# Fetching the context's rounded halves in the second cross attention, stored by the first

## Chip, cores and metric

The kernel runs on one core of a Trainium2 chip. The metric is the time of one execution on the device, in microseconds.

## What is computed

Six layers in a row work on `x` of shape (8, 64, 256), in float32. Two of them are cross attentions over the same context `ctx_1024` of shape (8, 1024, 256): the first layer, with a mask and a squared-relu norm, and the fourth, with a softmax. Cut to what matters:

```python
def _L0_xattn_ref(iQ, iK, mask, Wq, Wkv, Wo, nbias):          # H = 16, ADIM = 16
    rq = (iQ @ Wq.T).reshape(b, q, H, ADIM)
    kv = (iK @ Wkv.T).reshape(b, s, 2, H, ADIM)
    scores = einsum('bqhd,bshd->bhqs', rq, kv[:, :, 0]) / sqrt(ADIM)   # masked
    ...                                                        # relu, square, norm, values, Wo
def _L1_xattn_ref(query, key, value, w_q, w_k, w_v, w_o):     # 16 heads of 64
    scores = einsum('bhqd,bhkd->bhqk', query @ w_q, key @ w_k) * 64 ** -0.5
    attn = softmax(scores)
    return einsum('bhqk,bhkd->bhqd', attn, value @ w_v) ... @ w_o
x = x + _L0_xattn_ref(_layernorm(x), ctx_1024, mask, ...)
x = x + _L0_attn_ref(...);  x = x + _L0_ffn_ref(...)
x = x + _L1_xattn_ref(_layernorm(x), ctx_1024, ctx_1024, ...)
x = x + _L1_attn_ref(...);  x = x + _L1_ffn_ref(...)
```

## The kernel before

Each layer is a function with one block; inside it each engine has its own hand-written list of work, and semaphores tie the lists together. Products that need float32 precision from the faster float32r matmul are made of three matmuls (`product3`, L185): an operand is split into a rounded half `hi` (a cast, on ScalarE) and the remainder `lo` (raw minus `hi`, on VectorE or GpSimd), and hi x hi, hi x lo and lo x hi are added up.

The first cross attention is `xattn0` (L197). It goes batch by batch over the eight batches. SyncE loads the transposed context `ctxT` in two chunks of 128 features x 1024 positions (`load_chunk`, L261, 512 KB each) into one raw tile, once the halves of the batch before have been taken from it (L283, L284). ScalarE casts a chunk into `ctx_hi[b % 2]` (`split`, L320 to L324), VectorE subtracts into `ctx_lo[b % 2]` (`remainder`, L429 to L432), and TensorE makes keys and values from the halves (`piece`, L507) between the scores and outputs of the batch at work. The halves are two batches deep.

The second is `xattn1` (L1537). The key weights are absorbed into the queries, so the scores are queries against the transposed context itself, called the features, `cT[b % 2]` as `hi` and `lo`; the tiles of even batches are named e_cT, those of odd batches f_cT. The outputs are taken against the untransposed context, called the keys, `cN`. A batch has four groups g of two pairs of heads; G = 4 b + g counts groups, n counts pairs.

- SyncE (L1682 to L1732): per group `put` of two pairs (their probabilities, transposed in blocks by VectorE, go to a table `f_turned_rows` in device memory, 512 KB each, L1693), then `fetch` of the two (four transfers of 128 KB each bring them back into `pT_lo`, L1706). A fetch waits until its put has landed. Behind the fetches of group 2 the keys of the next batch are loaded (`load_keys`, L1573, 1 MB), behind those of group 3 the features of the batch after the next (`load_features`, L1569, 1 MB, into the raw tile `rawT`), for which SyncE first waits that the raw tile has been read (L1726, L1727). All of it is one queue.
- ScalarE: exponentials of the scores (L1600), the cast of fetched probabilities (`high`, L1785), and the casts of keys (L1776) and, in group 2, of features (L1769).
- GpSimd: the remainders of keys (L1749) and of features (`pool_features`, L1595).
- VectorE, for a group: `low` of the pairs fetched two groups ago (L1898), two maxima (L1605), and for each of two pairs the division and the block transpose (L1893).
- TensorE, for group G: scores of two pairs (24 matmuls of 512 columns, from `pe_scores`, L1615), then the outputs of group G - 2 (96 matmuls of 256 columns, `outputs`, L1983), which need the two `low` results. All are instructions of L189.

## Time and profile before

| | us |
|---|---|
| median of 3 runs | 962.04 |
| lowest, highest run | 959.30, 963.83 |
| the profiled execution | 959.08 |
| its span, first to last instruction | 957.4 |
| TensorE busy (matmuls) | 912.9 |
| VectorE busy | 632.9 |
| ScalarE busy | 500.1 |
| GpSimd busy | 196.7 |
| first cross attention, about | 0 to 192 |
| second cross attention, about | 377 to 815 |

The profile is one execution, so everything in it is read against 959.08 us and not against the median. Busy time of TensorE counts overlapping matmuls once. Transfers are not instructions of an engine: SyncE's rows show when a transfer is issued, and its landing is seen in what waits for it.

### The profile page before, as it was taken

Reading aid. Unit: us, or ns where it says so; the run is one execution under the profiler, and the core shown is the slowest. Engines: PE = TensorE matmul, PEld = TensorE weight load, DVE = VectorE, ACT = ScalarE, POOL = GpSimd, SP = SyncE. Lnnn points to the kernel's source line nnn. Section 1 sums busy time; section 2 is a strip of 40 time slices with the busy share of each in tenths; the row PEclk is TensorE's granted clock in tenths of the full one; section 3 lists DMA queues with packets and bytes.
Section 4 is the critical chain, followed back from the end, with each engine's and each line's share of the span. In section 5 each row is a group of like instructions: output and inputs, shape, how many; then the busy total and the mean of one; then the engine's idle time right before and its main releaser. Section 6 shows DMA issues by size and latency. Waiting matters only on the chain. (4 is left out here: it accounts for less than half of the span.)

```text
span 957.4 us, 20196 instructions
## 1 busy us (share of the span) xinstructions
PE 912.9 (95%) x8260; PEld 748.3 (78%) x8260; DVE 632.9 (66%) x866; ACT 500.1 (52%) x721; POOL 196.7 (21%) x190
## 2 busy tenths in 40 slices
PE   9999999888989999979999999999999999998996
PEld 7888888755679998558999999999989976567554
DVE  5667776768733335589897979898989843286221
ACT  5777777543456664655555564646454531312331
POOL 2000000020214441422131231404050211321101
PEclk9999999999979999999999999999999999997998
DMA  5211110020212222538887888787969870999993
GB/s 162 81 59 50 49 50 5 3 67 4 66 46 88 88 88 69 151 108 216 264 204 241 214 250 226 235 232 223 251 210 251 220 211 23 286 321 243 339 339 117
DMA packets 103848, 151.92 MB, mean 159 GB/s; under 512 B 11009, under 2 KB 84434, under 8 KB 103762
## 3 DMA queue, kind: packets, MB, share of 16 engines
q1 hardware_dynamic: 102930, 148.35, 53.5%
q0 software_dynamic: 832, 2.36, 0.8%
q8 instruction: 62, 1.02, 0.4%
q14 instruction: 24, 0.20, 0.1%
HBM read 114.50 MB, written 36.18 MB: 157 GB/s over the span
## 5 line engine op out<-in xcount | busy, mean ns | idle before, releaser
L189 PE MATMUL ps<-f_pT_lo,f_cN_hi 128*128 128x256 f32 x512 | 146.9, 287 | 0.0
L189 PE MATMUL ps<-f_pT_hi,f_cN_hi 128*128 128x256 f32 x512 | 145.2, 284 | 0.7 <-DVE f_pT_lo L1898 0.7
L189 PE MATMUL ps<-f_pT_hi,f_cN_lo 128*128 128x256 f32 x512 | 145.2, 284 | 0.0
L448 DVE SCALAR_TENSOR_TENSOR a_u<-ps,a_floor,a_cap 128x1024 f32<-128x1024 f32 x64 | 79.2, 1279 | 47.3 <-PE ps L543 46.9
L1749 POOL TENSOR_TENSOR f_cN_lo<-e_raw,f_cN_hi 128x512 fp32r<-128x512 f32 x32 | 48.4, 1541 | 260.7 <-ACT f_cN_hi L1776 260.7
L189 PEld LDWEIGHTS ps<-f_pT_hi,f_cN_hi 128*128 128x128 f32 x512 | 96.2, 188 | 4.0 <-DVE f_pT_lo L1898 2.2
L189 PEld LDWEIGHTS ps<-f_pT_hi,f_cN_lo 128*128 128x128 f32 x512 | 97.9, 191 | 0.0
L189 PEld LDWEIGHTS ps<-f_pT_lo,f_cN_hi 128*128 128x128 f32 x512 | 96.2, 188 | 1.0
L359 ACT ACTIVATE a_pr<-a_u,a_nb 128x1024 f32<-128x1024 f32 x64 | 73.8, 1153 | 42.7 <-DVE a_u L448 41.5
L1898 DVE TENSOR_TENSOR f_pT_lo<-f_pT_lo,f_pT_hi 128x1024 fp32r<-128x1024 f32 x64 | 81.1, 1290 | 20.0 <-ACT f_pT_hi L1785 19.9
L1785 ACT CAST f_pT_hi<-f_pT_lo 128x1024 fp32r<-128x1024 f32 x64 | 66.9, 1049 | 50.5 <-DMA f_pT_lo<-f_turned_rows 50.4
L1605 DVE TENSOR_REDUCE e_negmax<-ps 128x1 f32<-128x1024 f32 x64 | 76.6, 1217 | 17.4 <-PE ps L189 17.2
L1600 ACT ACTIVATE xn<-ps,e_negmax 128x1024 f32<-128x1024 f32 x32 | 35.7, 1116 | 95.6 <-DVE e_negmax L1605 95.6
L189 PE MATMUL ps<-e_cT_hi,e_qb_hi 128*128 128x512 f32 (+1 forms) x160 | 60.7, 379 | 4.7 <-ACT xn L1600 3.1
L189 PE MATMUL ps<-e_cT_hi,e_qb_lo 128*128 128x512 f32 (+1 forms) x160 | 59.7, 373 | 0.0
L189 PE MATMUL ps<-e_cT_lo,e_qb_hi 128*128 128x512 f32 (+1 forms) x160 | 59.4, 372 | 0.0
L1044 POOL TENSOR_TENSOR d_w_lo<-d_w,d_w_hi 128x512 fp32r<-128x512 f32 x32 | 41.3, 1289 | 78.0 <-ACT d_w_hi L1071 78.0
L189 PE MATMUL ps<-f_cT_hi,e_qb_lo 128*128 128x512 f32 x128 | 50.4, 394 | 0.0
L189 PE MATMUL ps<-f_cT_lo,e_qb_hi 128*128 128x512 f32 x128 | 50.2, 392 | 0.0
L189 PE MATMUL ps<-f_cT_hi,e_qb_hi 128*128 128x512 f32 x128 | 49.7, 388 | 0.0
L1110 DVE TENSOR_TENSOR d_h_lo<-d_h,d_h_hi 128x512 fp32r<-128x512 f32 x32 | 23.9, 746 | 36.8 <-ACT d_h_hi L1091 36.8
L1600 ACT ACTIVATE xnT<-ps,e_negmax 128x1024 f32<-128x1024 f32 x32 | 35.7, 1117 | 17.4 <-DVE e_negmax L1605 17.4
(414 smaller groups left out, 2193.0 us busy)
## 6 DMA issues: line engine op xcount, KB each, us to landing
f_turned_rows<-f_turned SPq DMA_DIRECT2D x64, 512.0 KB, 4.7
f_pT_lo<-f_turned_rows SPq DMA_DIRECT2D x256, 128.0 KB, 3.3
k_w<-in_L_ffn_W SPq DMA_DIRECT2D x30, 1024.0 KB, 14.6
a_ctxT<-in_ctxT SPq DMA_DIRECT2D x16, 512.0 KB, 4.8
d_w<-in_L_ffn_w SPq DMA_DIRECT2D x32, 256.0 KB, 2.7
e_raw<-in_ctxT SPq DMA_DIRECT2D x8, 1024.0 KB, 7.1
e_raw<-in_ctx SPq DMA_DIRECT2D x32, 256.0 KB, 5.9
k_b<-in_L_ffn_b SPq DMA_DIRECT2D x14, 256.0 KB, 11.8
```

Source lines behind the costliest of these rows:

```text
L189: last = nc.tensor.matmul(out, a[i], b[j], start=start and n == 0, stop=stop and n == 2, skip_group_check=skip)
L359: A.activation(pr[:, n % NP, :], u[:, n % NU, :], ACT.Square, bias=nb[:], scale=HD ** -0.5).then_inc(p_ready, 1)
L448: V.scalar_tensor_tensor(u[:, n % NU, :].rearrange("p (r w) -> p r w", r=RT), core.psum[:, 0:2048].rearrange("p (r w) -> p r w", r=RT)[:, ...
L1044: self.c.nc.gpsimd.tensor_tensor(lo[:], raw[:], hi[:].bitcast(F32), ALU.subtract).then_inc(self.lo[i], 1)
L1110: V.tensor_tensor(self.hp[1][:, f % self.RG, :], self.h[:, f % self.RH, :], self.hp[0][:, f % self.RG, :].bitcast(F32), ALU.subtract).then ...
L1600: nc.scalar.activation(pr[p % NPR], core.ps[p % 2][:], ACT.Exp, bias=negmax[:, p:p + 1], accum_out=total[:, p:p + 1]).then_inc(exp_ready, 1)
L1605: nc.vector.tensor_reduce(negmax[:, p:p + 1], core.ps[p % 2][:], AX, ALU.max, negate=True).then_inc(max_ready, 1)
L1749: nc.gpsimd.tensor_tensor(cN[1][:, ks, cols], raw[:, ks, cols], cN[0][:, ks, cols].bitcast(F32), ALU.subtract).then_inc(n_lo, 1)
L1785: nc.scalar.copy(moved(pT_hi, n), moved(pT_lo, n).bitcast(F32)).then_inc(hi_ready, 1)
L1898: nc.vector.tensor_tensor(moved(pT_lo, n), moved(pT_lo, n).bitcast(F32), moved(pT_hi, n).bitcast(F32), ALU.subtract).then_inc(lo_dve, 1)
```

## The change

`xattn0` gets a table in device memory, `halves_d`, of 2 halves x 8 batches x 2 chunks x 128 x 1024 floats (16.8 MB). Behind every chunk load SyncE stores the `hi` and the `lo` of the same chunk of the batch before (`keep`), two transfers of 512 KB; those of the last batch follow at the end, and SyncE waits for all of them. Before the halves' tiles are written again, ScalarE and VectorE wait for the stores of two batches before.

`xattn1` no longer loads raw features. `load_features` fetches the two halves from the table, two transfers of 1 MB, straight into `cT[b % 2]`. The casts and subtractions of features are gone, with their semaphores; TensorE waits for the landing itself. SyncE's waits on them are gone too; ahead of the load in group 3 it waits until all scores of the current batch are made, since the halves' tile is overwritten.

```diff
@@ -194,7 +194,7 @@
 
 
 
-def xattn0(core, x_d, ctxT_d, maskT_d, wqT_d, wkvT_d, woT_d, nbias_d):
+def xattn0(core, x_d, ctxT_d, maskT_d, wqT_d, wkvT_d, woT_d, nbias_d, halves_d):
     nc = core.nc
     H, HD = 16, 16
     HC = P // HD
@@ -246,6 +246,7 @@
         num_ready, den_psum, wo_in = sem("num_ready"), sem("den_psum"), sem("wo_in")
         v_ones, wo_zero, ident_ready = sem("v_ones"), sem("wo_zero"), sem("ident_ready")
         o_ready, y_psum, x_out = sem("o_ready"), sem("y_psum"), sem("x_out")
+        kept = [sem(f"kept{i}") for i in range(2)]
         split_count = lambda b, c: 2 * DC + DC * (b - 1) + c + 1
         norm = Norm(core, "a")
         ident, x = core.ident, core.x
@@ -262,6 +263,10 @@
 
             def load_mask(b):
                 sp.dma_start(mask_u8[:], maskT_d[b, :, :].rearrange("p (k t) -> p k t", t=T)).then_inc(mask_in, 16)
+
+            def keep(b, c):
+                sp.dma_start(halves_d[0, b, c, :, :], ctx_hi[b % 2][:, c, :].bitcast(F32)).then_inc(kept[b % 2], 16)
+                sp.dma_start(halves_d[1, b, c, :, :], ctx_lo[b % 2][:, c, :].bitcast(F32)).then_inc(kept[b % 2], 16)
 
             w_d = wkvT_d.rearrange("(c p) o -> p c o", p=P)
             sp.dma_start(wkv[:, :, 0:D], w_d[:, :, 0:D]).then_inc(wk_in, 16)
@@ -283,8 +288,15 @@
                     sp.wait_ge(hi_ready, 2 * DC if b == 1 else split_count(b - 1, c))
                     sp.wait_ge(lo_ready, 2 * DC if b == 1 else split_count(b - 1, c))
                     load_chunk(b, c)
+                    keep(b - 1, c)
                 sp.wait_ge(mask_read, b)
                 load_mask(b)
+            for c in range(DC):
+                sp.wait_ge(hi_ready, split_count(B - 1, c))
+                sp.wait_ge(lo_ready, split_count(B - 1, c))
+                keep(B - 1, c)
+            for i in range(2):
+                sp.wait_ge(kept[i], 32 * DC * (B // 2))
 
         @block.gpsimd
         def _(pool):
@@ -321,6 +333,7 @@
                 act.wait_ge(ctx_in[c], 16 * b + 16)
                 if b >= 2:
                     act.wait_ge(kv_psum, PIECES * (b - 1))
+                    act.wait_ge(kept[b % 2], 32 * DC * (b // 2))
                 A.copy(ctx_hi[b % 2][:, c, :], ctxT[:, c, :]).then_inc(hi_ready, 1)
 
             def queries(b):
@@ -428,6 +441,8 @@
 
             def remainder(b, c):
                 dve.wait_ge(hi_ready, split_count(b, c))
+                if b >= 2:
+                    dve.wait_ge(kept[b % 2], 32 * DC * (b // 2))
                 V.tensor_tensor(ctx_lo[b % 2][:, c, :], ctxT[:, c, :], ctx_hi[b % 2][:, c, :].bitcast(F32),
                                 ALU.subtract).then_inc(lo_ready, 1)
 
@@ -1534,7 +1549,7 @@
 
 
 
-def xattn1(core, a, finished, early):
+def xattn1(core, a, finished, early, halves_d):
 
 
     nc = core.nc
@@ -1551,7 +1566,7 @@
         rawT = both[:, 0:DC * S].rearrange("p (c s) -> p c s", s=S)
         raw = both[:, DC * S:DC * S + KT * D].rearrange("p (k d) -> p k d", d=D)
         cT = [[core.sb("e_cT0_" + n, [P, DC, S], F32R, ctx) for n in ("hi", "lo")]]
-        t_in, n_in, t_hi, t_lo = core.sem("e_t_in"), core.sem("e_n_in"), core.sem("e_t_hi"), core.sem("e_t_lo")
+        t_in, n_in = [core.sem(f"e_t{i}_in") for i in range(2)], core.sem("e_n_in")
         NPR = 2
         HALF = HP // 2
         QD = 32
@@ -1566,7 +1581,9 @@
         norm = Norm(core, "e")
 
         def load_features(sp, b):
-            sp.dma_start(rawT[:], a["ctxT"][b, :, :].rearrange("(c p) k -> p c k", p=P)).then_inc(t_in, 16)
+            for i in range(2):
+                sp.dma_start(cT[b % 2][i][:].bitcast(F32), halves_d[i, b, :, :, :].rearrange("c p k -> p c k")
+                             ).then_inc(t_in[b % 2], 16)
 
         def load_keys(sp, b):
             for j in range(4):
@@ -1586,14 +1603,6 @@
             dve.wait_ge(qb_hi, 2 * b + half + 3)
             nc.vector.tensor_tensor(qb[1][:, :, cols], queries_of(b, half), qb[0][:, :, cols].bitcast(F32),
                                     ALU.subtract).then_inc(qb_lo, 1)
-
-        def pool_features(pool, b):
-            hi, lo = cT[b % 2]
-            for i in range(4):
-                c, cols = i // 2, slice(S // 2 * (i % 2), S // 2 * (i % 2 + 1))
-                pool.wait_ge(t_hi, 2 * b + c + 1)
-                nc.gpsimd.tensor_tensor(lo[:, c, cols], rawT[:, c, cols], hi[:, c, cols].bitcast(F32),
-                                        ALU.subtract).then_inc(t_lo, 1)
 
         def act_exponentials(act, b, p):
             act.wait_ge(max_ready, HP * b + p + 1)
@@ -1614,7 +1623,7 @@
 
         def pe_scores(pe, b, p):
             if p == 0:
-                pe.wait_ge(t_lo, 4 * b + 4)
+                pe.wait_ge(t_in[b % 2], 32 * (b // 2) + 32)
             if b == 0 and p % 2 == 0:
                 pe.wait_ge(qb_lo, p // 2 + 1)
             if b >= 1 and p % HALF == 0:
@@ -1707,7 +1716,6 @@
                                      rows[n % SLOTS, :, S // 4 * j:S // 4 * (j + 1)].rearrange("(i k) w -> k i w", k=QD)
                                      ).then_inc(pT_in[n % 2], 16)
 
-                sp.wait_ge(t_lo, 4)
                 load_features(sp, 1)
                 for b, g in groups:
                     G = NG * b + g
@@ -1723,9 +1731,8 @@
                         else:
                             sp.dma_start(wo, a["L1_xattn_w_o"].rearrange("(h p) o -> p h o", p=P)).then_inc(wo_in, 16)
                     if g == 3 and b + 1 < B:
-                        sp.wait_ge(t_hi, 2 * b + 4)
-                        sp.wait_ge(t_lo, 4 * b + 8)
                         if b + 2 < B:
+                            sp.wait_ge(s_psum, HP * (b + 1))
                             load_features(sp, b + 2)
                         else:
                             sp.dma_start(wv, a["L1_xattn_w_v"].rearrange("(c p) o -> p c o", p=P)).then_inc(v_in, 16)
@@ -1739,7 +1746,6 @@
                     ps = slice(2 * i, 2 * i + 2)
                     nc.gpsimd.tensor_tensor(wk2[1][:, ps, :], wk[:, ps, :], wk2[0][:, ps, :].bitcast(F32),
                                             ALU.subtract).then_inc(wk_lo, 1)
-                pool_features(pool, 0)
                 early.gpsimd()
 
                 def keys(b, c):
@@ -1755,19 +1761,11 @@
                     if b >= 1:
                         keys(b, 0)
                         keys(b, 1)
-                    if b + 1 < B:
-                        pool_features(pool, b + 1)
                 pool.wait_ge(wo_hi, 1)
                 nc.gpsimd.tensor_tensor(wo2[1], wo, wo2[0].bitcast(F32), ALU.subtract).then_inc(wo_lo, 1)
 
             @block.scalar
             def _(act):
-                def features(b, c):
-                    act.wait_ge(t_in, 16 * b + 16)
-                    if b >= 2:
-                        act.wait_ge(s_psum, HP * (b - 1))
-                    nc.scalar.copy(cT[b % 2][0][:, c, :], rawT[:, c, :]).then_inc(t_hi, 1)
-
                 def keys(b, c):
                     act.wait_ge(n_in, 64 * b + 64)
                     if b >= 1:
@@ -1828,10 +1826,8 @@
                 weights(3)
                 evict(0)
                 query(3)
-                features(0, 0)
                 evict(1)
                 query(4)
-                features(0, 1)
                 evict(2)
                 first_queries(0)
                 query(5)
@@ -1857,9 +1853,6 @@
                     if g == 2:
                         if b >= 1:
                             keys(b, 1)
-                        if b + 1 < B:
-                            features(b + 1, 0)
-                            features(b + 1, 1)
                     if g == 3 and b + 1 < B:
                         queries(b + 1, 0)
                     if g == 0:
@@ -2873,13 +2866,14 @@
 def program(nc, a, out):
     with ExitStack() as ctx:
         core = Core(nc, ctx)
+        halves = nc.dram_tensor("ctx_halves", (2, B, DC, P, S), F32).ap()
         xattn0(core, a["x"], a["ctxT"], a["maskT"], a["L0_xattn_Wq"], a["L0_xattn_Wkv"], a["L0_xattn_Wo"],
-               a["L0_xattn_nbias"])
+               a["L0_xattn_nbias"], halves)
         memory0(core, a)
         ffn0(core, a)
         finished = core.retire_sems()
         early = Ahead(core, "k", a["L1_ffn_W1"])
-        xattn1(core, a, finished, early)
+        xattn1(core, a, finished, early, halves)
         kept = (early.w1_in, early.zeroed, early.zero_out)
         finished = [s for s in core.retire_sems() if s not in kept]
         attn1_ffn1(core, a, out, early, finished)
```

## Rows read from the trace of the kernel before

**Rows 1.** Stretches: bounds; length, PE, PEld, DVE, ACT, POOL busy; clock, DMA share, GB/s.

```profile
100.00:140.00 40.00, 39.71 (x840) 34.29 (x829) 31.94 (x30) 30.13 (x40) 0.00 (x0) 1.00 0.18 59
...
382.00:386.00 4.00, 4.00 (x10) 1.81 (x11) 0.69 (x1) 2.81 (x5) 0.28 (x1) 1.00 1.06 391
...
427.20:430.60 3.40, 3.40 (x10) 2.66 (x9) 3.15 (x5) 2.98 (x5) 0.00 (x0) 0.51 0.44 141
...
451.65:723.77 272.12, 271.82 (x1730) 247.43 (x1729) 236.06 (x251) 150.65 (x204) 71.86 (x48) 1.00 0.83 232
...
555.00:560.00 5.00, 5.00 (x27) 4.25 (x26) 3.75 (x4) 2.66 (x4) 0.00 (x0) 1.00 1.00 338
```

**Rows 2.** Odd batches' feature tiles by instruction: duration ns min/median/max, first and last start.

```profile
L1595 POOL TENSOR_TENSOR f_cT_lo<-e_raw,f_cT_hi x16: 1282/1521/2257, 431.1 to 714.3; 128x512 fp32r<-128x512 f32 x16
L1769 ACT CAST f_cT_hi<-e_raw x8: 1042/1044/1051, 430.0 to 706.7; 128x1024 fp32r<-128x1024 f32 x8
```

**Rows 3.** `low` by duration; and TensorE's waits: us in total, times, longest.

```profile
L1898 DVE TENSOR_TENSOR f_pT_lo<-f_pT_lo,f_pT_hi x64: 1181/1215/2309, 431.0 to 781.7; 128x1024 fp32r<-128x1024 f32 x64
...
PE ps L189 <- ACT xn L1600: 3.1, 1, 3.1
...
PE ps L189 <- DVE f_pT_lo L1898: 0.7, 2, 0.4
```

**Rows 4.** Batch 1's chunks in the first attention: issue, landing of L261, casts.

```profile
9.41 0.82 SPq L261 DMA_DIRECT2D a_ctxT<-in_ctxT  x2
...
DMA to landing us min/median/max: 4.4/4.7/6.1
...
18.09 2.00 ACT L324 CAST a_ctx_hi<-a_ctxT 128x1024 fp32r<-128x1024 f32 x2
```

**Rows 5.** One batch change: landing of all puts (L1693), SyncE's issues, ScalarE's cast.

```profile
DMA to landing us min/median/max: 2.6/4.7/8.5
...
551.83 0.40 SPq L1569 DMA_DIRECT2D e_raw<-in_ctxT  x1
552.45 2.51 SPq L1693 DMA_DIRECT2D f_turned_rows<-f_turned  x2
560.32 3.94 SPq L1706 DMA_DIRECT2D f_pT_lo<-f_turned_rows  x8
...
564.88 1.05 ACT L1785 CAST f_pT_hi<-f_pT_lo 128x1024 fp32r<-128x1024 f32 x1 [3.02 <-DMA f_pT_lo<-f_turned_rows]
```

**Rows 6.** VectorE's second `low` of group 0, six batches: start, duration.

```profile
476.14 1.48 DVE L1898 TENSOR_TENSOR f_pT_lo<-f_pT_lo,f_pT_hi 128x1024 fp32r<-128x1024 f32 x1 [0.76 <-ACT f_pT_hi L1785]
...
523.39 1.69 DVE L1898 TENSOR_TENSOR f_pT_lo<-f_pT_lo,f_pT_hi 128x1024 fp32r<-128x1024 f32 x1 [1.79 <-ACT f_pT_hi L1785]
...
568.25 1.23 DVE L1898 TENSOR_TENSOR f_pT_lo<-f_pT_lo,f_pT_hi 128x1024 fp32r<-128x1024 f32 x1 [1.07 <-ACT f_pT_hi L1785]
...
612.06 1.46 DVE L1898 TENSOR_TENSOR f_pT_lo<-f_pT_lo,f_pT_hi 128x1024 fp32r<-128x1024 f32 x1 [0.79 <-ACT f_pT_hi L1785]
...
657.82 2.23 DVE L1898 TENSOR_TENSOR f_pT_lo<-f_pT_lo,f_pT_hi 128x1024 fp32r<-128x1024 f32 x1 [1.27 <-ACT f_pT_hi L1785]
...
704.43 1.56 DVE L1898 TENSOR_TENSOR f_pT_lo<-f_pT_lo,f_pT_hi 128x1024 fp32r<-128x1024 f32 x1 [0.68 <-ACT f_pT_hi L1785]
```

**Rows 7.** TensorE's first output matmul of the same groups: start, duration.

```profile
479.78 0.28 PE L189 MATMUL ps<-f_pT_hi,f_cN_hi 128*128 128x256 f32 x1
...
525.13 0.39 PE L189 MATMUL ps<-f_pT_hi,f_cN_hi 128*128 128x256 f32 x1
...
570.44 0.28 PE L189 MATMUL ps<-f_pT_hi,f_cN_hi 128*128 128x256 f32 x1
...
615.65 0.28 PE L189 MATMUL ps<-f_pT_hi,f_cN_hi 128*128 128x256 f32 x1
...
660.89 0.28 PE L189 MATMUL ps<-f_pT_hi,f_cN_hi 128*128 128x256 f32 x1
...
706.11 0.33 PE L189 MATMUL ps<-f_pT_hi,f_cN_hi 128*128 128x256 f32 x1
```

## The prediction

> **What bounds the kernel now.** I read busy time by stretch first, then the producers and consumers of the edited tiles, then SyncE's transfers and the two engines behind them, batch by batch.
>
> The second cross attention is where work is taken away, so its limit decides what that is worth. Over six whole batches of it TensorE is busy 271.82 of 272.12 us, at full clock; VectorE has 236 us, ScalarE 151, GpSimd 72, and the 16 DMA engines a share of 0.83 [rows 1]. A batch is a sixth of that: 45.4 us, with VectorE at 39, ScalarE at 25 and GpSimd at 12. The reader is to see two things: TensorE alone sets the pace, and what stands nearest behind it is not GpSimd or ScalarE but the transfers and the chain that hangs on them. The first cross attention is dense on TensorE too (39.71 of 40.00 us), with the DMA engines at 0.18 [rows 1].
>
> **What is taken away.** Per batch: four GpSimd subtractions at a median of 1.5 us and two ScalarE casts at 1.04 us; in all at most 32 x 1.5 = 48 us of GpSimd and 16 x 1.04 = 17 us of ScalarE [rows 2]. Neither bounds [rows 1], so these 65 us are worth nothing by themselves. Two side effects can be worth something. VectorE's remainder of the probabilities takes 1.2 us at the median and 2.3 at most [rows 3]; the long ones lie beside GpSimd's subtractions. One less of them is 1.1 us of VectorE a batch, where it has 6 us spare. TensorE has waited for that remainder only twice, 0.7 us in all [rows 3]; with the refill of its pipeline I put the recovery at 0.9 us, bounds 0 and 1.5. The Trainium skill (SBUF — State Buffer, on the port pair that VectorE and GpSimd share) says that a VectorE instruction with two SBUF inputs and a GpSimd one that reads SBUF exclude each other; the trace agrees (2.3 against 1.2 us), and the page would change nothing in the sum.
>
> The start of the second attention also has stalls of TensorE, 3.1 us the longest, waiting for an exponential [rows 3]. That exponential waits for a maximum behind VectorE's query remainders, which run beside the GpSimd subtractions of the keys. Those stay, so I take nothing from it.
>
> **What is added in the first attention.** 32 stores of 512 KB on SyncE's queue, two behind each chunk load, and three new waits. Three transfers' worth of bytes replace one, so the share of 0.18 rises to about 0.5: not a bound. The tightest place is the second chunk of batch 1. Both chunks go out from 9.41 us on [rows 4]; two stores now stand between them, 1 MB, 2.7 us at the rate below plus two issues. The chunk's landing, at most 6.1 us after issue so far [rows 4], moves from about 16 to about 19 us. ScalarE casts it as the second instruction of the pair that starts at 18.09 us, thus at 19.1 [rows 4]: a delay of 0 to 1 us, and TensorE needs its halves only after eight query matmuls. I take 0, bound 1 us, once. Later chunks have a batch's time. The new waits on the stores ask about a batch (21 us) after they are issued, and hold up nobody: behind ScalarE's wait stand the squares for TensorE, behind VectorE's the clamps, but a 512 KB store has landed long before. The last stores and SyncE's last wait lie some 45 us ahead of the stage's end. All that: 0, bounds 0 and 1 us.
>
> **What is added in the second attention.** A batch's features were one transfer of 1 MB and become two, 2 MB, on the same queue, at the same place: behind the fetches of group 3 and ahead of the puts of the next group. SyncE needs 0.4 us more to issue, hidden while the queue is full. The wait put in front (all scores of the batch) has been met when SyncE gets there, since the second put before it already waits for the last pair's transposed probabilities. So it costs nothing, and nothing behind it waits.
>
> The bytes are the cost. Take the batch change at 552 us [rows 5]: features at 551.83 us, the first put of the next group at 552.45. That put has landed when its fetch goes out, at 560.32 us: 7.9 us. Of all puts the quickest took 2.6 us, the median one 4.7 [rows 5]. The transfers run in the order of issue, and the DMA engines stand at 1.00 from 555 to 560 us [rows 1]. One more megabyte ahead of the put makes it land later by its own length. How long is that? The two rates for 4 KB rows are 391 GB/s (382 to 386 us, nearly all of it such loads) and 338 GB/s (555 to 560 us, mixed) [rows 1]: 1.05 MB by these is 2.7 or 3.1 us. I take 2.7, since the added transfer is purely of 4 KB rows. An estimate by the fit in the Trainium skill (DMA: Bandwidth & Descriptors, Anatomy of one DMA) would be 2.4 us for the bytes; with it the sum below would be 1.8 us smaller.
>
> From there it goes on without a cushion: the fetch starts when the put has landed, ScalarE's cast starts when the fetch has landed (it sat idle 3.02 us for it), VectorE's subtraction follows, and TensorE's output matmuls of that group need the result [rows 5, 6]. How early is that result now? End of the second subtraction against the first output matmul, for the six batch changes behind which features are loaded [rows 6, 7]:
> - 477.62 against 479.78: 2.16 us early
> - 525.08 against 525.13: 0.05
> - 569.48 against 570.44: 0.96
> - 613.52 against 615.65: 2.13
> - 660.05 against 660.89: 0.84
> - 705.99 against 706.11: 0.12
>
> 2.7 us later, TensorE stalls 0.54 + 2.65 + 1.74 + 0.57 + 1.86 + 2.58 = 9.9 us; with 3.1 us it is 12.3. A stall moves TensorE and so all that follows, but the next batch change meets the same cushion afresh, so the stalls add. The following group has recovered: its VectorE chain loses the GpSimd contention (1.1 us), and TensorE itself comes 0.5 to 2.7 us later. The load of the last weights at the seventh batch change stays 1 MB. The first two feature loads stand before any put. The features of batch 0 are complete one transfer length (2.7 us) later than the raw ones were, but skip two casts and four subtractions (8 us in a row) on their way to TensorE, which is still projecting queries then. They cost 0. So the edit trades idle engines' time for a second megabyte on the one resource with no room at that moment.
>
> **Sum.** Profiled execution 959.08 us (span 957.4): + 9.9 (stalls) - 0.9 (VectorE contention) + 0 (first attention) = 968.1 us. The profiled execution lies 3.0 us under the median of the runs, 962.04, and the edit adds 9.0 us to either: forecast 971.0 us for the median. Its own range goes from 2.7 us a transfer with 1.5 us recovered (+8.4) to 3.1 us with nothing recovered and 1 us in the first attention (+13.3); with the 2 us by which the runs scatter on either side, 968 to 977 us.
>
> **Rivals.**
> - *The transfer is absorbed.* The DMA engines are idle 17% of a batch, 7.7 us [rows 1]. If the put's landing is set by issue or by the round trip of its own completion, and not by the bytes ahead, the megabyte goes into the gaps. The shift stays under 1 us, only three changes are tight at all, and the recovered 0.9 us nearly pays: -1 to +4 us, 961 to 966, as a point 962 us. This is the case that is not slower; it decides if the put behind the features lands less than about 1 us later than now. Against it: share 1.00 right there, and 7.9 against 2.6 us [rows 1, 5].
> - *It costs more.* After the 3.1 us stall TensorE ran 3.4 us at a granted clock of 0.51, its 1.2 GHz level [rows 1, 3]. Three of my stalls are about 2.6 or 1.9 us. If each brought the clock down like that, the price is about 1.6 us each (eight matmuls at 0.43 in place of 0.23 us); with the groups behind tight as well, another 1 us a batch: 5 + 6 on top, 982 us. Against it: no stall of that length stands in these batches, so nothing shows that one under 3 us is enough.
> - *Freed engines give more than I see.* The starting stalls shrink, 3 to 6 us: 957 us. Against it: the chain named above does not contain the removed work.
> - *The first attention pays*, for stores that hold the chunk loads: TensorE waits a little over 0.5 us a batch, 4 us, and the second is absorbed: 966 us. Against it: 21 us a batch with an idle queue.
>
> **How the numbers follow.** Forecast 0.56, absorbed 0.24, costs more 0.12, first attention pays 0.03, freed engines give more 0.05. A measurement of this kernel can tell about 0.5% from no change: 957.2 to 966.9 us. The absorbed case and the first-attention case lie within it (0.27), the forecast and the dearer case above (0.68), the last below (0.05). For 8 in 10 the range takes the forecast's own range and the absorbed case, 961 us, and part of the dearer one, 978 us.
>
> **What would show it.** GpSimd's and ScalarE's busy time down by some 45 and 17 us; written bytes up by 17 MB, in the first attention. Stalls of TensorE ended by VectorE's remainder of the probabilities, once a batch, at the first output matmul of the group after the features, 0.5 to 3 us each. ScalarE's wait for the fetch there 2 to 3 us longer, the put's way from 7.9 to over 10 us, the DMA share of a batch near 0.9. No remainder of 2.3 us in the group after the tight one. I am wrong if the put's way grows by under 1 us, if TensorE stays without gaps over whole batches, or if it waits in the first attention.

## The result, and the profile after

The changed kernel takes 966.55 us (median of 16 runs, 963.28 to 972.67), the kernel before 958.33 us in the 16 runs beside them. The two medians stand 8.2 us apart. The ratio, which is what the text goes by from here on, is 1.0077, with a 95% interval from 1.0053 to 1.0101: 7.4 us slower, 5 to 10. Put to the median of 962.04 us that was shown ahead, that is 969.4 us, where 971.0 had been forecast. The profiled execution took 966.18 us, its span went from 957.4 to 964.5 us.

In the changed kernel `low` is L1891, `high` L1783, `put` L1702, `fetch` L1715, the halves' loads L1585, and the first attention's cast of the context L337.

TensorE's waits between 430 and 790 us, changed kernel (waited for; us in total, times, longest). It is the only line:

```profile
PE ps L189 <- DVE f_pT_lo L1891: 6.8, 6, 2.6
```

And the six, each the first output matmul of group 0 of a batch, as those of [rows 7]; in brackets the idle time before it and what ended it:

```profile
479.84 0.39 PE L189 MATMUL ps<-f_pT_hi,f_cN_hi 128*128 128x256 f32 x1 [0.40 <-DVE f_pT_lo L1891]
...
527.24 0.39 PE L189 MATMUL ps<-f_pT_hi,f_cN_hi 128*128 128x256 f32 x1 [1.92 <-DVE f_pT_lo L1891]
...
572.90 0.39 PE L189 MATMUL ps<-f_pT_hi,f_cN_hi 128*128 128x256 f32 x1 [0.18 <-DVE f_pT_lo L1891]
...
619.66 0.39 PE L189 MATMUL ps<-f_pT_hi,f_cN_hi 128*128 128x256 f32 x1 [1.28 <-DVE f_pT_lo L1891]
...
667.78 0.39 PE L189 MATMUL ps<-f_pT_hi,f_cN_hi 128*128 128x256 f32 x1 [2.61 <-DVE f_pT_lo L1891]
...
713.66 0.39 PE L189 MATMUL ps<-f_pT_hi,f_cN_hi 128*128 128x256 f32 x1 [0.39 <-DVE f_pT_lo L1891]
```

Six stalls, one at each batch change with a halves' load ahead of it, and none elsewhere. The same batch change as in [rows 5], SyncE's issues and then the two engines of the chain, changed kernel:

```profile
553.32 0.43 SPq L1585 DMA_DIRECT2D e_cT_hi<-ctx_halves  x1
554.09 0.38 SPq L1585 DMA_DIRECT2D e_cT_lo<-ctx_halves  x1
554.58 1.52 SPq L1702 DMA_DIRECT2D f_turned_rows<-f_turned  x2
563.61 4.03 SPq L1715 DMA_DIRECT2D f_pT_lo<-f_turned_rows  x8
...
568.29 1.05 ACT L1783 CAST f_pT_hi<-f_pT_lo 128x1024 fp32r<-128x1024 f32 x1 [4.33 <-DMA f_pT_lo<-f_turned_rows]
...
571.57 1.28 DVE L1891 TENSOR_TENSOR f_pT_lo<-f_pT_lo,f_pT_hi 128x1024 fp32r<-128x1024 f32 x1 [0.96 <-ACT f_pT_hi L1783]
```

From put to fetch it is 9.0 us here, 7.9 before; over the six changes 8.6 to 10.8 with a mean of 9.9, where before has 6.6 to 8.5 with a mean of 7.5: 2.4 us more. ScalarE's idle time for the fetch is 4.3 to 6.8 us in place of 1.5 to 3.9.

The stretches of [rows 1] that matter, changed kernel (length, busy time of PE, PEld, DVE, ACT, POOL; clock, DMA share, GB/s):

```profile
100.00:140.00 40.00, 38.93 (x873) 33.51 (x875) 30.60 (x29) 29.33 (x40) 0.00 (x0) 1.00 0.43 151
451.65:723.77 272.12, 265.34 (x1674) 239.95 (x1673) 222.11 (x244) 136.45 (x186) 36.84 (x24) 1.00 0.85 249
```

In the second, GpSimd has half its work left and ScalarE 14 us less, and TensorE is idle 6.78 us in place of 0.30. The clock stays at full speed (1.00, the 2.4 GHz level). In the first, TensorE is idle 1.07 us, which it was not before (0.29). That is a loss in the first attention, for which I had put down nothing.

### The profile page after: what moved, and what is told of

The parts are those of the page before. It is cut to its first block and busy times, and to the rows that moved or that the text cites. A ratio compares the mean times of both kernels' runs of the same rounds, so it can differ in the third digit from the quotient of the medians.

```text
span 964.5 us, 20185 instructions
## 1 busy us (share of the span) xinstructions
PE 911.6 (95%) x8260; PEld 745.4 (77%) x8260; DVE 623.2 (65%) x866; ACT 486.1 (50%) x705; POOL 149.5 (16%) x158
## 3 DMA queue, kind: packets, MB, share of 16 engines
q8 instruction: 62, 1.02, 0.4%
HBM read 122.89 MB, written 52.95 MB: 182 GB/s over the span
## 5 line engine op out<-in xcount | busy, mean ns | idle before, releaser
L1783 ACT CAST f_pT_hi<-f_pT_lo 128x1024 fp32r<-128x1024 f32 x64 | 67.1, 1048 | 76.1 <-DMA f_pT_lo<-f_turned_rows 76.0
L1891 DVE TENSOR_TENSOR f_pT_lo<-f_pT_lo,f_pT_hi 128x1024 fp32r<-128x1024 f32 x64 | 76.6, 1218 | 35.1 <-ACT f_pT_hi L1783 35.1
```

Source lines behind the costliest of these rows:

```text
L1783: nc.scalar.copy(moved(pT_hi, n), moved(pT_lo, n).bitcast(F32)).then_inc(hi_ready, 1)
L1891: nc.vector.tensor_tensor(moved(pT_lo, n), moved(pT_lo, n).bitcast(F32), moved(pT_hi, n).bitcast(F32), ALU.subtract).then_inc(lo_dve, 1)
```

## Where the time goes: the first attention

The second attention starts at 377.09 us, 0.2 us later than before (376.91), and by that the first one had cost nothing. But TensorE's granted clock dips at another time in every execution, and a dip hides such a sum. So a marker is needed up to which the clock is full in both: the last cast of a context chunk, the second one of batch 7. Kernel before, then changed kernel:

```profile
141.18 1.05 ACT L324 CAST a_ctx_hi<-a_ctxT 128x1024 fp32r<-128x1024 f32 x1
```

```profile
144.60 1.05 ACT L337 CAST a_ctx_hi<-a_ctxT 128x1024 fp32r<-128x1024 f32 x1
```

3.4 us later. Part of it lies at the very start, changed kernel:

```profile
11.45 0.43 SPq L268 DMA_DIRECT2D ctx_halves<-a_ctx_hi  x1
...
12.81 1.08 DVE L118 BATCH_NORM_STATS2 stats<-resid 128x6 f32<-128x256 f32 x3 [1.24 <-DMA resid<-in_x]
```

`x` is used from 12.81 us on, before the change from 10.34, though it was issued at 2.87 and 2.86 us. The first store is issued at 11.45 us, but the lateness is older than that: ScalarE casts the second half of batch 0's context from 9.02 us on, before the change from 7.38. ScalarE has copies of keys to make behind the layer norm of `x`, and TensorE waits for one of them:

```profile
15.69 0.36 PE L189 MATMUL ps<-a_wkv_hi,a_ctx_hi 128*128 128x256 f32 x1 [1.35 <-ACT a_kT L354]
```

Later there are small gaps of TensorE in the changed kernel that end with nothing which the profile shows ("issue"):

```profile
139.88 0.75 PE L578 MATMUL ps<-a_pr,a_v 128*32 128x64 f32 x36 [0.77 <-issue]
```

Every experiment below has a profile, so these signs can be read in fourteen executions. Four are of kernels without these stores (the kernel before twice, before with its load moved, and the one with 4 of 32 stores): the marker stands at 141.18, 141.69, 142.16 and 141.22 us. Ten are of kernels that store everything: it stands at 142.08 to 144.60, mean 143.43. On average that is 1.9 us later. It has two parts, and there are two places to cut between them. `x` is used from 10.34 to 11.74 us without stores (mean 10.9) and from 10.97 to 12.81 with them (mean 12.0); these overlap, so this 1.1 us may be scatter of the executions. From the use of `x` to the marker it takes 130.4 to 130.8 us without and 130.8 to 131.8 us with stores, mean 131.4: 0.8 us more, with hardly an overlap, and "issue" gaps of 0.2 to 0.8 us stand in nine of the ten and in none of the four. A cut behind the start, where TensorE begins the scores of batch 0, is sharper. Kernel before, then changed kernel:

```profile
25.40 0.45 PE L543 MATMUL ps<-a_qd,a_kT 32*128 32x128 f32 x5 [0.17 <-ACT a_qd L330]
```

```profile
27.48 0.39 PE L558 MATMUL ps<-a_qd,a_kT 32*128 32x128 f32 x4 [0.17 <-ACT a_qd L343]
```

From there to the marker it takes 115.8 us in each of the four without stores (they agree within 0.01 us) and 116.1 to 117.1 us in the ten with them, mean 116.8. So the stores cost 1.0 us behind the start, or 1.9 us if the late start is theirs too. The new waits are not the reason: in the first attention no idle time of ScalarE or VectorE is ended by a store's landing, only SyncE's last wait is.

What the gaps are can be followed one step further. They stand at the same two matmuls in every execution that has them, near 96 and 139 us. The profile lists an "instruction" queue (q8, 62 packets, 1.02 MB), whose packets of 16 KB are spread over the span. From the start of the packet ahead of the later matmul to TensorE's last wait ahead of it (for `a_oT`, at 138.47 us in the changed kernel, 136.11 before) it is 2.4 to 2.8 us in the four executions without stores and 0.8 to 1.7 us in the ten with them. The shorter this lead, the longer the gap: 0.77 us at a lead of 0.8, 0.5 to 0.56 at 1.0 to 1.2, 0.23 at 1.5 and 1.6, none at 1.6 and 1.7. That fits instructions which arrive late beside the stores' traffic. No run changed that alone, so it is not shown.

## The experiments

### The stores alone

The second attention is the one of before; the first is the changed one. In this and the following sections the edits are cut to their main lines and stand against the changed kernel, where nothing else is said.

```diff
-        xattn1(core, a, finished, early, halves)
+        xattn1(core, a, finished, early)
```

> The first cross attention of the changed kernel (32 stores, three waits on them) with the second of the kernel before, which loads and splits raw features. Theory (the whole price lies in the second attention's six batch changes): the ratio to the kernel before is 1.000, 0 to +1 us, and TensorE's first output matmul of the second attention lies within 1 us of that of before. Rival, the stores cost in the first attention: +4 us or more, with gaps of TensorE before 190 us. In the profile of the changed kernel the first 15 us lay 2.07 us later, before any store was issued, and had been regained by 377 us; by the theory this is no effect of the stores, and may or may not be seen again here; if the stores' program causes it, resid x lands near 12.8 us here too in place of 10.3.

Measured: 1.0037 of the kernel before (0.9999 to 1.0075). That leaves 0 to 7 us; the marker stands at 142.08 us here, 0.5 us behind the mean of those without stores. `x` is used from 11.32 us, between my two values. The profile held a second surprise: its second attention is that of the kernel before, and yet TensorE waited for the remainders of the probabilities four times, 4.1 us in all, where [rows 3] had 0.7 us.

### The fetches alone

```diff
-                    keep(b - 1, c)
+                    if b == 1:
+                        keep(0, c)
-            sp.dma_start(cT[b % 2][i][:].bitcast(F32), halves_d[i, b, :, :, :]...
+            sp.dma_start(cT[b % 2][i][:].bitcast(F32), halves_d[i, 0, :, :, :]...
```

> The changed kernel with the stores of batch 0 alone (4 of 32), and every batch of the second attention fetches these halves, so that its scores are taken against batch 0's features: the second attention's cost without the first's. With the changed kernel at 1.008 and the stores alone at 1.0037 (0.9999 to 1.0075), the stores' own price is open between 0 and 3 us. If they cost nothing: 1.007 to 1.009 and the same 7 to 9 us of waits for the remainders. If they cost 3 us: 1.004 to 1.005. The first window: if the table or the stores shift the start of the kernel, x lands near 10.3 us here and near 12.8 us where all is stored.

Measured: 1.0042 (1.0010 to 1.0073), against 1.0081 with all stores. TensorE's waits for the remainders are 8.3 us, like those of the changed kernel. So the second attention's price is there without the stores, and the stores' own price is the difference, 0.39% or 3.7 us; with these intervals 0 to 8 us, and 1.0 to 1.9 us by the marker. My first theory had them at 0 to 1 us: the low end of this at best. `x` is used from 10.38 us here.

### One half in place of two

```diff
-            for i in range(2):
+            for i in range(2 if b < 2 else 1):
                 sp.dma_start(cT[b % 2][i][:].bitcast(F32), halves_d[i, b, :, :, :]...
```

> The changed kernel, but from batch 2 on only the hi half is fetched behind group 3's fetches: 1 MB as before the change, with all its waits and its order as they are. The lo tile keeps the remainders of batch 0 or 1, so this part of the scores is of another batch. Theory (the second megabyte delays the put): the way from put to fetch issue at the six batch changes goes back from 9.9 to about 7.5 us, TensorE's six waits for the remainder of the probabilities go down from 6.8 us to under 1 us in total, and the time is that of before or up to 1 us less: ratio 0.999 to 1.000. Rival, the delay comes with the new wait, the two issues or the missing raw tile and not with the bytes: the stalls stay at 5 us or more, ratio near 1.007.

Measured: 0.9944 (0.9906 to 0.9981). TensorE between 430 and 790 us:

```profile
PE ps L189 <- DVE f_pT_lo L1891: 0.9, 1, 0.9
```

That one wait is at 435.81 us, in batch 0; none of the six is left, and from put to fetch it is 5.3 to 8.1 us, mean 6.9, where the changed kernel has 9.9. Waits and order are those of the changed kernel, and the one issue that is missing lies ahead of the put, from which the way is counted. So the stalls come from the bytes. Against the changed kernel's 1.0081 (measured again below) the second megabyte costs 1.37%, 13 us (9 to 18). TensorE's waits in the profiles account for 6 to 8 us of that, about 1 us at each change: the put comes 3.0 us later, and the cushions take the rest. The miss is the other side: I had expected 0 to 1 us under before and got 5.4. With all the stores in it, that kernel is further ahead than the one profile of before, with its 0.7 us of waits, allowed.

### A third megabyte

```diff
                             load_features(sp, b + 2)
+                            if b >= 1:
+                                sp.wait_ge(more, 16 * b)
+                            sp.dma_start(rawT[:], a["ctxT"][b + 2, :, :]...).then_inc(more, 16)
```

> The changed kernel with a third transfer of 1 MB behind the two halves at the same six batch changes, the raw features into a tile that nothing reads: extra traffic only. Theory: every stall of TensorE there is longer by the length of one such transfer, 2.4 us, 14 us over the changed kernel and 21 to 22 us over before, ratio 1.022 (1.020 to 1.025); put to fetch issue goes from 9.9 to 12.3 us. Rival, gaps of the DMA engines absorb further bytes, so that the cost is not one for one: 5 us or less over the changed kernel. Rival, longer stalls of 3 to 5 us bring TensorE's granted clock down: another 1.5 us for each, +30 us over before.

Measured: 1.0233 (1.0164 to 1.0302), as expected. Put to fetch 11.2 to 13.0 us, mean 12.1; the waits:

```profile
PE ps L189 <- DVE f_pT_lo L1897: 21.5, 6, 5.3
```

and the longest of them:

```profile
584.39 0.58 PE L189 MATMUL ps<-f_pT_hi,f_cN_hi 128*128 128x256 f32 x1 [5.27 <-DVE f_pT_lo L1897]
```

That is 12.8 to 14.7 us over the changed kernel's 8.7 and 6.8, 2.1 to 2.5 us a change, as much as the put's way grows by (2.3 us): the third megabyte is paid for in full, since the second has used up the cushions. One, two and three megabytes ahead of the put stand at 0.9944, 1.0081 and 1.0233, about 14 us for each. That looks like one price for every megabyte, and is not. In the profiles the second adds 6 to 8 us of waits and the third 13 to 15; that the times show equal steps lies within their intervals, the first step's being 9 to 18 us. The rival on the clock is true here as well. The stretch behind the longest stall:

```profile
584.40:587.80 3.40, 3.40 (x16) 3.40 (x17) 3.13 (x4) 2.23 (x4) 2.30 (x2) 0.50 1.06 216
```

The granted clock is 0.50, the 1.2 GHz level. Behind the four stalls of 3.8 to 5.3 us it is 0.50 to 0.59, behind one of 2.26 us 0.53, behind one of 2.33 us 1.00. So the 14.6 us over the changed kernel are not all stall; how they divide was not measured apart, and the profiled execution (989.8 us) lies above its kernel's median.

### Both kernels again, on one chip

No edit: the kernel before and the changed kernel, each profiled a second time.

> The kernel before once more, profiled a second time. In the second series the kernel with one half fetched was 5 us faster than before, where I had expected 0 to 1, and the same second attention showed four stalls of 4.1 us in one execution and none of them in another. Reading A: the six cushions of before (2.2 to 0.05 us in its one profile) scatter from execution to execution by a microsecond or so, so that before itself stalls 2 to 5 us in most executions behind the remainders of the probabilities, 0.7 us in the profiled one was a good draw, and their places differ. Then this profile shows 2 to 5 us of such waits. Reading B: before stalls under 1 us as a rule, and the 5 us come from elsewhere. The ratio to before is 1.000 by any reading, and its interval says how far a ratio here can be trusted.

> The changed kernel once more, on the chip of the experiments. With one half it was 0.9944, with three transfers 1.0233; if each megabyte costs the same, two are at 1.008. Theory: 1.007 to 1.009, 5 to 10 us of TensorE's waits for the remainders at the six batch changes. A rival that has the removal worth only 1 us and the stores worth the rest would put it at 1.010 or more.

Measured: before against itself 1.0019 (0.9986 to 1.0052), the changed kernel 1.0081 (1.0055 to 1.0108). The waits between 430 and 790 us, before and then changed:

```profile
PE ps L189 <- DVE f_pT_lo L1898: 4.7, 7, 1.3
```

```profile
PE ps L189 <- DVE f_pT_lo L1891: 8.7, 6, 1.9
```

Reading A holds: the same program had 0.7 us of such waits in one execution and 4.7 us in another, and with the stores ahead of it 4.1. The time of the whole execution doesn't show it: the two of before took 959.08 and 959.15 us. What the second lost in this stage it did not lose elsewhere, where TensorE's clock dipped less (the mean granted clock is 0.987 against 0.978). The executions with 4.7 and 4.1 us of waits are 2.6 and 2.3 us under the medians of their own kernels, so that on average before may well wait more than the 3.2 us which the three make. The changed kernel has 6.8 and 8.7 us, all at the six changes. From put to fetch the second execution of before takes 8.3 us on average (7.5 in the first), that of the changed kernel 9.9 again.

### GpSimd's subtractions put back

```diff
+                def same_work(b):
+                    for i in range(4):
+                        ...
+                        nc.gpsimd.tensor_tensor(rawT[:, c, cols], rawT[:, c, cols], rawT[:, c, cols],
+                                                ALU.subtract).then_inc(worked, 1)
```

on top of the kernel with one half.

> The kernel with one half fetched (1 MB a batch, ratio 0.9944; the scores of batches 2 to 7 use remainders of another batch), and GpSimd's subtractions of features put back as work without a user: four of 128x512 a batch, behind the keys' remainders, on a tile that nothing reads. Transfers and ScalarE stay as they are. If the 5 us of that kernel come from VectorE, whose remainders are no longer drawn out to over 2 us by GpSimd, they go: ratio 0.998 to 1.001, remainders of 2.2 us and more again in the group after the tight one. If they come from ScalarE's two casts less, or from the loads that go out 1 us earlier since SyncE's waits on the split are gone, the ratio stays at 0.993 to 0.996.

Measured: 0.9976 (0.9945 to 1.0007), against 0.9944 without that work. 3.1 us, in the middle between the two answers; the two ratios are from different chips, and their intervals overlap. The waits go from 0.9 to 3.5 us and VectorE's remainders from 80.5 to 82.2 us in total, which speaks for the contention being part of the 5 us, but this is not shown.

### The same two megabytes in other places

Both halves behind group 1's fetches of the next batch:

```diff
-                            sp.wait_ge(s_psum, HP * (b + 1))
-                            load_features(sp, b + 2)
+                    if g == 1 and b >= 1 and b + 1 < B:
+                        sp.wait_ge(s_psum, HP * b)
+                        load_features(sp, b + 1)
```

> The changed kernel with the same 2 MB a batch, but the fetch of both halves stands behind group 1's fetches of the following batch in place of group 3's (where the scores that read the tile are done as well, and the DMA engines' share was 0.4 to 0.5 in the kernel before). The last projection weights stay where they are. Theory (what costs is that the second megabyte stands ahead of the put of group 0, the only put whose chain has no cushion): puts at the batch change go to 5 to 6 us, the six stalls vanish, and the time is 0 to 2 us under that of before, ratio 0.998 to 1.000. If group 2's chain has less cushion than I read, it stalls there in its place: 2 to 5 us over before. Rival, the total of bytes a batch costs wherever they stand (DMA share 0.85 to 0.90): +4 to +8 us, ratio 1.004 to 1.008.

Measured: 1.0001 (0.9962 to 1.0039). The six stalls are gone, and five of about 1 us stand elsewhere:

```profile
PE ps L189 <- DVE f_pT_lo L1891: 4.3, 5, 1.1
```

The puts of group 0 now take 3.8 us on average to their fetch, those of group 2, behind the halves, 7.2. Between the theory's two cases.

One half behind group 0's fetches, the other behind group 1's:

```diff
+                    if g < 2 and 1 <= b < B - 1:
+                        sp.wait_ge(s_psum, HP * b)
+                        load_features(sp, b + 1, (g,))
```

> The changed kernel with its 2 MB spread: the hi half of the next batch behind group 0's fetches, the lo half behind group 1's, the keys behind group 2's as before, nothing behind group 3's; the value weights behind group 1's fetches of the last batch. So no put has more than 1 MB ahead of it. Both halves moved behind group 1 gave 1.000, with five stalls of about 1 us behind them. Theory (what costs is the bytes ahead of one put against the cushion of its chain, not their total): no put way over 7.5 us but behind the keys, stalls under 1 us in total, the time of the kernel with one half: ratio 0.993 to 0.997. Rival, the total of bytes costs (share 0.85 in place of 0.83): 1.000 to 1.004.

Measured: 1.0041 (1.0008 to 1.0075), at the rival's upper end. Four waits, 4.6 us; the puts of groups 1, 2 and 3 take 6.3, 6.7 and 6.8 us, each with a megabyte ahead. SyncE at one batch change:

```profile
560.04 0.43 SPq L1585 DMA_DIRECT2D e_cT_hi<-ctx_halves  x1
561.24 2.51 SPq L1702 DMA_DIRECT2D f_turned_rows<-f_turned  x2
570.27 3.64 SPq L1715 DMA_DIRECT2D f_pT_lo<-f_turned_rows  x8
```

Spreading the bytes over three puts did not make them free.

The same lines four lines higher, between the two puts and the two fetches of groups 0 and 1:

```diff
                     put(2 * G)
                     put(2 * G + 1)
+                    if g < 2 and 1 <= b < B - 1:
+                        sp.wait_ge(s_psum, HP * b)
+                        load_features(sp, b + 1, (g,))
                     fetch(2 * G)
```

> As the spread version (hi half in group 0, lo half in group 1, keys behind group 2's fetches, value weights in group 1 of the last batch), but each half is issued between the group's puts and its fetches and not behind the fetches. There SyncE waits at least 2.6 us for the puts to land, in which these transfers can run. Spread was 1.0041 with 4.6 us of waits. Theory (the cost is bytes that stand ahead of a put or fetch while it could run; bytes that fill the wait for the put's landing are free): 0.995 to 1.000, waits under 2 us. Rival, the DMA engines are as good as full and any further megabyte pushes the chain by its length: 1.003 to 1.008, fetches land later by about what the puts gain.

Measured: 0.9955 (0.9925 to 0.9985), 4.3 us faster than the kernel before. SyncE at one batch change, then the stretch of the stage (columns as above):

```profile
549.12 2.52 SPq L1702 DMA_DIRECT2D f_turned_rows<-f_turned  x2
551.70 0.42 SPq L1585 DMA_DIRECT2D e_cT_hi<-ctx_halves  x1
552.22 4.49 SPq L1715 DMA_DIRECT2D f_pT_lo<-f_turned_rows  x8
```

```profile
430.00:790.00 360.00, 359.32 (x2304) 324.52 (x2304) 295.66 (x322) 182.55 (x247) 51.73 (x29) 1.00 0.88 247
```

From put to fetch it is 3.1 us (9.0 in the changed kernel), and TensorE is idle 0.68 of 360 us (6.78). The same 2 MB are moved, and the DMA engines have a larger share than ever (0.88). The two last kernels differ in nothing but the side of the fetches on which the load is issued. Directly behind a put SyncE has to wait for its landing, and a transfer issued there runs in that wait; directly behind a fetch it stands ahead of the next put.

From ScalarE's queue:

```diff
                     if g == 0:
                         queries(b, 1)
+                        if b + 1 < B:
+                            act.wait_ge(s_psum, HP * b)
+                            load_features(nc.scalar, b + 1)
```

> The changed kernel with the halves issued from ScalarE's queue, at the head of group 0 of the next batch (ScalarE has waited for those scores by then), some 5 us later than SyncE issued them and behind the puts. Two things change: the puts don't stand behind the halves on one queue, and ScalarE issues for about 1 us a batch. If the order on the one queue is what costs: put ways at the batch change of 7 us or less, and 0.996 to 1.001. If it is the share of the DMA engines: the fetches of group 0 run against the halves and land later, the waits stay at 5 us or more, 1.005 to 1.010.

Measured: 1.0068 (1.0031 to 1.0106), waits of 9.9 us. The edit did not do what I said of it:

```profile
547.36 0.37 ACTq L1585 DMA_DIRECT2D e_cT_hi<-ctx_halves  x1
547.76 0.50 ACTq L1585 DMA_DIRECT2D e_cT_lo<-ctx_halves  x1
...
551.79 3.74 SPq L1715 DMA_DIRECT2D f_pT_lo<-f_turned_rows  x8
556.31 2.52 SPq L1702 DMA_DIRECT2D f_turned_rows<-f_turned  x2
```

ScalarE reaches the head of group 0 nine microseconds before the put of that group, not behind it, and so the halves run against the fetches of group 3. Put to fetch fell only from 9.9 to 8.2 us. The transfers of another queue take the same engines' time: the rival is right in that. The Trainium skill (DMA: Bandwidth & Descriptors, Issuing engines are not separate DMA queues) says the same of DMAs started by different engines. What the queue alone would do with the place unchanged is not told by this run.

### The place without the change

```diff
                     put(2 * G)
                     put(2 * G + 1)
+                    if g == 0 and 1 <= b < B - 1:
+                        sp.wait_ge(t_hi, 2 * b + 2)
+                        sp.wait_ge(t_lo, 4 * b + 4)
+                        load_features(sp, b + 1)
                     fetch(2 * G)
```

Here the edit stands against the kernel before; it also takes the old load away behind the fetches of group 3.

> The kernel before, nothing of the change in it, with its one transfer of raw features moved by one step: out between the puts and the fetches of group 0 of the next batch in place of behind the fetches of group 3 (value weights in the same gap of group 1 of the last batch). The changed kernel with its two halves in such gaps was 0.9955 of before, against 1.0041 with the same halves just behind the fetches of the same groups. Question: how much of the 0.9955 is the place and how much the change. By the prices so far, the change in a place where its bytes are free has 2 us of stores against it and up to 3 us of GpSimd's subtractions for it. If that holds, this kernel is within 2 us of 0.9955: 0.994 to 0.998, waits for the remainders under 2 us in place of the 0.7 to 4.7 us of before. Rival, the gain needs the change (freed engines): 0.999 to 1.001.

Measured: 0.9939 (0.9917 to 0.9962), 5.9 us faster than before. TensorE between 430 and 790 us:

```profile
PE ps L189 <- DVE f_pT_lo L1899: 0.4, 1, 0.4
```

and the stretch:

```profile
430.00:790.00 360.00, 359.53 (x2289) 324.04 (x2288) 305.68 (x326) 194.71 (x262) 90.62 (x57) 1.00 0.83 230
```

GpSimd and ScalarE do all their old work (90.62 and 194.71 us), and within the intervals it is no slower than the changed kernel in its best place. So the gain of 0.9955 needs nothing of the change; it comes with the place. The pair is not exact: this kernel moves one transfer into one gap, the other two halves into two, and they ran on different chips.

A stretch of the stage without the rest of the kernel says how much of the times lies there: from the first output matmul of group 3 in batch 0 to that of group 3 in batch 7, all at full clock but for those marked.

| kernel | stretch, us | TensorE's waits in it, us |
|---|---|---|
| before, two executions | 315.5, 321.6 | 0.3, 4.9 |
| stores alone | 317.9 | 2.0 |
| before, load in the gap | 315.0 | 0.0 |
| changed, two executions | 323.1, 324.8 | 6.8, 8.7 |
| few stores (clock drops in it) | 326.0 | 7.4 |
| one half | 314.7 | 0.0 |
| one half, GpSimd's work put back | 317.0 | 1.7 |
| three megabytes (clock drops in it) | 345.7 | 21.5 |
| both halves behind group 1 | 320.4 | 4.3 |
| spread, behind the fetches | 320.5 | 4.6 |
| spread, in the gaps | 314.7 | 0.0 |
| ScalarE's queue | 324.5 | 8.0 |

Kernels without waits meet at 314.7 to 315.0 us. The three executions with the old second attention average 318.3 us, the two changed ones 323.9: the stage's own price is 5.6 us by these. The load in the gap gains 3.3 us here against that average, and of its 5.9 us the rest is not located.

## Why the prediction was right, point by point

- *TensorE bounds the second attention, freed engines are worth nothing by themselves.* Right: its idle time is what moved, and the last kernel gets the gain with all of the freed work put back.
- *The second megabyte stands ahead of group 0's put and delays it by its length.* Right, and shown from both sides: with one megabyte no stall at the six changes, with three 13 to 15 us of waits more. The term was 2.7 us, with 3.1 as its bound. From put to fetch the changed kernel takes 2.4 us longer than the first execution of before and 1.6 us longer than the second; against its neighbours it is 3.0 us from one megabyte to two and 2.3 us from two to three. So 2.7 lies within what was measured, and the scatter is too large to tell it from the estimate of 2.4 us by the Trainium skill (DMA: Bandwidth & Descriptors, Anatomy of one DMA) that was written beside it; the trace agrees with either.
- *The stalls, 9.9 us from six cushions.* Six stalls at the six named matmuls, but 6.8 us in all, and 8.7 in the second execution. Single ones were off by up to 2 us either way: 1.28 us where I had 0.57, 0.39 where I had 2.58. The step that fails is to take a cushion of one execution for a property of the kernel. In the same program they change by a microsecond or two from one execution to the next, so that 0.7 us of waits in the first profile of before were 4.7 in the second.
- *The recovery, 0.9 us.* Too small, in the same step: with one megabyte and the subtractions gone the kernel is 5 us faster than before, in part since before had more stalls to lose than its profile showed (3.2 us of waits on average, against 0.9 with one megabyte). Long remainders of 2.3 us, which were to vanish behind the tight group, did vanish in the changed kernel's first execution (1.56 us at most); in the second there is one of 2.35 us, and with both halves in group 1 eleven of 2.2 us and more, so they were displaced and not removed.
- *The first attention, 0 with a bound of 1 us.* At the bound or over it: 1.0 us behind the start, 1.9 with it. ScalarE did not wait for the chunk that I had named, in any of the fourteen executions; what I had not looked for were TensorE's small gaps without a named cause. That TensorE waits in the first attention was one of the signs of being wrong, and it did wait, 1.35 us at 15.69. But before with its load moved, which has no store, waits 0.6 us at the same matmul.
- *The sum.* 9.9 - 0.9 + 0 = 9.0 us against 7.4 (5 to 10). By what the profiles show on average it is 7.8 - 3.2 = 4.6 us of waits in the second attention and 1.9 in the first, 6.5 us; with the 5.6 us of the stage's stretch in place of the waits it is 7.5 us. The mechanism and its place were right. Its terms were each off by 1 to 2 us, with signs that cancel in part, and that the sum came as close as it did is luck to that extent. Of the signs, GpSimd's busy time fell by 47.2 us, ScalarE's by 14.0, and the bytes written to device memory rose from 36.18 to 52.95 MB, as said; the DMA share of the stage rose to 0.85 only, where near 0.9 was expected.
- *The rivals.* Absorbed: the put's way grew by 2.4 us (1.6 against the second execution of before) and not by less than 1, and part of it was absorbed, by the cushions. The clock: it stayed at 1.00 in all six stalls of the profile, up to 2.61 us. With three megabytes a drop comes behind five of six stalls, one of them of 2.26 us only.

What stays open: whether the start is later in the kernels with stores by chance or for a reason, since it is so before the first store is issued (the cast at 9.02 us for 7.38; on average 8.5 for 7.9, and the two groups overlap), and whether the "issue" gaps are instructions that come late. Nor was it tried whether fewer and larger stores, or stores in other places of the first attention, cost less.

## What to carry to other kernels

A transfer is paid for by what stands behind it in its queue. Before adding bytes, look at which round trip comes next, and issue them where the queue has to wait for a landing anyway: the same 2 MB, spread over two groups, stood at +0.4% behind the fetches, ahead of the next put, and at −0.5% between puts and fetches, and moving one line of the kernel before gained nearly what the whole change had lost. And a cushion of a tenth of a microsecond read in one execution is no cushion and no stall, but a draw; where the forecast hangs on it, profile the unchanged kernel a second time, and compare stages by a marker up to which the clock is full in both kernels.

## What was not expected of the hardware

The DMA engines were no bound at a share of 0.88 over 360 us and were one at 0.85, with TensorE idle 0.68 and 6.78 us: the share alone doesn't tell. The same kernel waited 0.7 and 4.7 us for the same producer in two executions. Stalls of TensorE of 2.26 and 2.33 us in the same execution were followed by a granted clock of 0.53 and 1.00. And adding 32 stores of 512 KB, with the DMA share at 0.37 to 0.46 between 30 and 130 us and no computing engine waiting for a store, still set TensorE back by 1 to 2 us in 140, in part in gaps at the same two matmuls, whose length goes with how late a packet of the "instruction" queue starts.
